# W2 and beta loaded second and multiplied first on TensorE, in a two-layer hypergraph block

## The reference

```python
def hypergraph_conv(x, adj, W, b):
    H = (adj != 0).astype(x.dtype)
    w = adj.reshape(N, -1)[:, :C]
    xw = jnp.einsum('ncd,hd->nch', x, W)
    Dn = jnp.einsum('nce,ne->nc', H, w)
    Dn = jnp.where(Dn > 0, 1.0 / Dn, 0.0)
    Be = H.sum(axis=1)
    Be = jnp.where(Be > 0, 1.0 / Be, 0.0)
    m = Be[:, :, None] * jnp.einsum('nce,nch->neh', H, xw)
    out = Dn[:, :, None] * jnp.einsum('nce,neh->nch', H, m)
    return out + b

h = jnp.maximum(_layernorm(x, axis=-1), 0.0)
a = jax.nn.relu(hypergraph_conv(h, adj, W1, b1))
a = layer_norm(a, gamma, beta)
x = x + (hypergraph_conv(a, adj, W2, b2) + h)
```

## Time and profile before

| | us |
|---|---|
| median of 3 runs (639.63 to 640.46) | 640.25 |
| the profiled execution | 639.93 |
| its span | 638.1 |
| TensorE (PE) busy | 619.6 |
| VectorE (DVE) busy | 475.1 |
| ScalarE (ACT) busy | 290.3 |
| GpSimd (POOL) busy | 110.9 |

### The profile page before, as it was taken

One profiled execution on the slowest core, in us unless ns is written; L12 is line 12 of the kernel. 1 busy time (PEld: TensorE's weight loads), 2 busy tenths in 40 slices (PEclk: granted clock), 3 DMA queues, 4 the chain that ended last, 5 costly groups with the idle time before them and its releaser, 6 DMA issues.

```text
span 638.1 us, 11993 instructions
## 1 busy us (share of the span) xinstructions
PE 619.6 (97%) x4808; PEld 467.1 (73%) x4808; DVE 475.1 (74%) x1148; ACT 290.3 (45%) x540; POOL 110.9 (17%) x132
## 2 busy tenths in 40 slices
PE   2999799999999999999999999999999999999998
PEld 1756658688586885778766886768858688586887
DVE  6899878976689765995779948798478876388632
ACT  4464935373435635364353632646335373125620
POOL 0114019422210304004040040401212012000000
PEclk9999999999999999999999999999999999999999
DMA  8995680169810696108951099213990159000701
GB/s 336 257 349 106 124 339 2 33 126 187 348 34 2 151 222 288 34 1 201 250 211 34 22 225 299 116 34 82 203 357 21 34 115 207 10 1 2 196 3 67
DMA packets 146215, 89.78 MB, mean 141 GB/s; under 512 B 134896, under 2 KB 135536, under 8 KB 141168
## 3 DMA queue, kind: packets, MB, share of 16 engines
q1 hardware_dynamic: 146160, 89.02, 51.6%
HBM read 47.06 MB, written 8.39 MB: 87 GB/s over the span
## 4 chain that ended last, share of the span: by engine, by line
PE 92%; DVE 4%; ACT 2%; DMA 1%; issue 0%
PE acc L582 18%; PE acc L599 18%; PE acc L522 15%; PE acc L563 12%; PE acc L543 11%; PE acc L502 7%; PE acc L504 7%; PE acc L484 2%; PE acc L443 1%; PE acc L445 1%; DVE z L937 1%; DMA z<-z_split_ring 1%; ACT z_split_ring L671 1%; ACT z L672 1%; DMA x_in<-x 1%; DVE incidence L873 1%
## 5 line engine op out<-in xcount | busy, mean ns | idle before, releaser
L582 PE MATMUL acc<-xw_split,incidence 128*128 128x256 f16 x1024 | 113.2, 273 | 0.0
L599 PE MATMUL acc<-edge_means,incidence_t 128*128 128x256 f16 x1024 | 113.1, 273 | 0.0
L582 PEld LDWEIGHTS acc<-xw_split,incidence 128*128 128x128 bf16 x1024 | 100.1, 98 | 13.2 <-DVE xw_split L973 0.2
L599 PEld LDWEIGHTS acc<-edge_means,incidence_t 128*128 128x128 bf16 x1024 | 100.2, 98 | 13.1
L629 ACT ACTIVATE edge_means<-acc,edge_inverse 128x256 f16<-128x256 f32 x128 | 55.2, 472 | 116.1 <-PE acc L582 68.4
L502 PE MATMUL acc<-h_split,incidence 128*128 128x257 f16 x448 | 98.6, 273 | 0.0
L504 PE MATMUL acc<-h_split,incidence 128*128 128x256 f16 x448 | 98.6, 273 | 0.0
L522 PE MATMUL acc<-incidence_t,edge_means 128*128 128x512 bf16 x448 | 97.8, 379 | 0.0
L563 PE MATMUL acc<-w_split,z 128*128 128x256 f16 x768 | 85.5, 273 | 3.5 <-DMA z<-z_split_ring 3.5
L563 PEld LDWEIGHTS acc<-w_split,z 128*128 128x128 f16 x768 | 74.9, 98 | 13.1 <-DVE edge_means L1024 2.7
L543 PE MATMUL acc<-w_split,pt_split 128*128 128x512 f16 x384 | 84.2, 379 | 0.0
(11 more groups left out here) (104 smaller groups left out, 639.4 us busy)
## 6 DMA issues: line engine op xcount, KB each, us to landing
adj_in<-adj SPq DMA_DIRECT2D x32, 1024.0 KB, 10.2
out<-residual SPq DMA_DIRECT2D x32, 256.0 KB, 2.6
x_in<-x SPq DMA_DIRECT2D x7, 1024.0 KB, 5.5
edge_weights<-adj SPq DMA_DIRECT2D x7, 512.0 KB, 3.7
x_in<-x SPq DMA_DIRECT2D x2, 512.0 KB, 4.6
z<-w1t SPq DMA_DIRECT2D x1, 512.0 KB, 12.5
xw_split<-w2t SPq DMA_DIRECT2D x1, 512.0 KB, 13.2
incidence_t<-incidence SPq DMA_TRANSPOSE x32, 4.8
```

Source lines behind the costliest of these rows:

```text
L582: last = nc.tensor.matmul(acc[:, 0:DOUT], inc[:, b.slot, ct, P * et:P * (et + 1)], xw[:, ct, part, :], start=(ct == 0 and part == HI), sto ...
L599: last = nc.tensor.matmul(acc[:, 0:DOUT], inc_t[:, b.slot, ct, et, :], edge[:, et, part, :], start=(et == 0 and part == HI), stop=(et == T ...
```

## The change

W2 and beta are issued second and third on SP, ahead of the second half of x. beta has its own semaphore, so GpSimd need not wait for gamma. `bias_times_w2` is the first work on TensorE, cut into two halves of 128 columns that go into banks 6 and 7 at columns 264 to 391, beside the sums of the first stage A (columns 0 to 256). The degrees go to bank 5. On VectorE, the inverse root of the lower half of x comes directly after its variance, two of the upper half's four `bn_stats` go behind the first `h0_lo`, the upper variance goes behind the second `h0_lo`, and `split_weights` goes behind the first `factor`.

```diff
--- before.py
+++ after.py
@@ -91,7 +91,8 @@
     Z_BEHIND = 2
     ZRING = 6
     RING = 8
-    BIAS_BANK, DEGREE_BANK = 7, 6
+    BIAS_BANK, DEGREE_BANK = 6, 5
+    BIAS_AT = LO_AT
     WPARTS = 3
     CT_FIRST = 6
     PER_BATCH = 5 * T + 4
@@ -183,6 +184,8 @@
         def u_group(b, g):
             return res[:, b.slot, GT * g:GT * (g + 1), :] if b.offset < 2 else u[:, g % 2, :, :]
 
+        bias_sums = acc_ring[:, BIAS_BANK:BIAS_BANK + 2, BIAS_AT:BIAS_AT + P]
+
         def counts(b, half):
             at = place("A", b, T // 2 * half)
             return acc_ring[:, at:at + T // 2, ONE]
@@ -193,6 +196,7 @@
         adj_loaded = [sem(f"adj_loaded{q}") for q in range(QUARTERS)]
         x_first = sem("x_first")
         weights_loaded = sem("weights_loaded")
+        beta_loaded = sem("beta_loaded")
         w1_loaded = sem("w1_loaded")
         rows_loaded = sem("rows_loaded")
         stored = [sem(f"stored{q}") for q in range(QUARTERS)]
@@ -341,14 +345,14 @@
             b0, nxt = Batch(0, 0), Batch(0, 1)
             x_rows = rows(x, b0)
             sp.dma_start(x_in[:, 0:T // 2, :], x_rows[:, 0:T // 2, :]).then_inc(x_first, 16)
+            sp.dma_start(w2f, w2t.rearrange("(t p) o -> p t o", p=P)).then_inc(w2_loaded, 16)
+            sp.dma_start(gb[:, 1, :], beta).then_inc(beta_loaded, 16)
             sp.dma_start(x_in[:, T // 2:T, :], x_rows[:, T // 2:T, :]).then_inc(x_loaded, 16)
             for q in range(QUARTERS):
                 load_adj(b0, q)
-            sp.dma_start(gb[:, 1, :], beta).then_inc(weights_loaded, 16)
             sp.dma_start(gb[:, 0, :], gamma).then_inc(weights_loaded, 16)
             sp.dma_start(w_col[:, 0, :], first_weights).then_inc(col_loaded, 16)
             sp.dma_start(w1f, w1t.rearrange("(t p) h -> p t h", p=P)).then_inc(w1_loaded, 16)
-            sp.dma_start(w2f, w2t.rearrange("(t p) o -> p t o", p=P)).then_inc(w2_loaded, 16)
             sp.dma_start(b2_row[:, :], b2.to_broadcast([P, DOUT])).then_inc(b2_loaded, 16)
             for q in range(2):
                 sp.wait_ge(inc_ready, QT * (q + 1))
@@ -398,7 +402,7 @@
                     nc.gpsimd.tensor_tensor(res[:, b.slot, t, :], x_in[:, t, :], b2_row[:, :],
                                             ALU.add).then_inc(res_ready, 1)
 
-            pool.wait_ge(weights_loaded, 32)
+            pool.wait_ge(beta_loaded, 16)
             for ht in range(HT_):
                 last = nc.gpsimd.tensor_copy(beta_cols[:, ht, :], gb[:, 1, ht:ht + 1].to_broadcast([P, P]))
             last.then_inc(beta_ready, 1)
@@ -448,11 +452,13 @@
                         last.then_inc(a_done, 1)
 
             def bias_times_w2():
+
                 pe.wait_ge(beta_ready, 1)
                 pe.wait_ge(w2_loaded, 16)
-                for ht in range(HT_):
-                    last = nc.tensor.matmul(acc_ring[:, BIAS_BANK, 0:DOUT], beta_cols[:, ht, :], w2f[:, ht, :],
-                                            start=(ht == 0), stop=(ht == HT_ - 1))
+                for half in range(2):
+                    for ht in range(HT_):
+                        last = nc.tensor.matmul(bias_sums[:, half, :], beta_cols[:, ht, :],
+                                                w2f[:, ht, P * half:P * (half + 1)], start=(ht == 0), stop=(ht == HT_ - 1))
                 last.then_inc(bias_done, 1)
 
             def first_degrees():
@@ -468,8 +474,6 @@
             def first_stage_b():
                 b = Batch(0, 0)
                 for half in range(2):
-                    if half == 1:
-                        bias_times_w2()
                     for q in (2 * half, 2 * half + 1):
                         pe.wait_ge(inc_t_ready[q], 16)
                     if half == 1:
@@ -530,10 +534,10 @@
                 for t in range(T):
 
                     pe.wait_ge(pt_ready, b.count(4, 2 * (t // 4 + 1)))
+                    if isinstance(b.loop, int) and b.offset == 0 and place("C", b, t) == BIAS_BANK:
+                        pe.wait_ge(bias_read, 1)
                     if isinstance(b.loop, int) and b.offset == 0 and place("C", b, t) == DEGREE_BANK:
                         pe.wait_ge(deg_read, 1)
-                    if isinstance(b.loop, int) and b.offset == 0 and place("C", b, t) == BIAS_BANK:
-                        pe.wait_ge(bias_read, 1)
                     if not (isinstance(b.loop, int) and b.offset == 0):
                         pe.wait_ge(t2_ready, b.next(-1).count(T, t + 1))
                     acc = bank("C", b, t)
@@ -602,6 +606,7 @@
                     last.then_inc(f_done, 1)
 
 
+            bias_times_w2()
             first_stage_a()
             first_stage_b()
             stage_c(Batch(0, 0))
@@ -755,7 +760,7 @@
             for g in range(GROUPS // 2, GROUPS):
                 relu_tiles(b0, g)
                 h0_hi_part(b0, g)
-            act.wait_ge(weights_loaded, 32)
+            act.wait_ge(weights_loaded, 16)
             act.wait_ge(w2_loaded, 16)
             for ht in range(HT_):
                 last = copy(gf[:, ht, :], w2f[:, ht, :], scale=gb[:, 0, ht:ht + 1])
@@ -1070,15 +1075,16 @@
             for t in range(T // 2):
                 V.bn_stats(stat[:, t, :], x_in[:, t, :]).then_inc(x_stat, 1)
             variance(x_ln, x_stat, x_half, b0, X_STEPS, DIN, lower)
+            inverse_root(x_ln, x_half, b0, X_STEPS, 1.0, lower)
             dve.wait_ge(x_loaded, 16)
-            for t in range(T // 2, T):
+            for t in range(T // 2, T // 2 + 2):
                 V.bn_stats(stat[:, t, :], x_in[:, t, :]).then_inc(x_stat, 1)
-                if t == T // 2 + 1:
-                    inverse_root(x_ln, x_half, b0, X_STEPS, 1.0, lower)
             incidence(b0, 0)
             h0_lo(b0, 0)
+            for t in range(T // 2 + 2, T):
+                V.bn_stats(stat[:, t, :], x_in[:, t, :]).then_inc(x_stat, 1)
+            h0_lo(b0, 1)
             variance(x_ln, x_stat, x_step, b0, X_STEPS, DIN, upper)
-            h0_lo(b0, 1)
             inverse_root(x_ln, x_step, b0, X_STEPS, 1.0, upper)
             incidence(b0, 1)
             h0_lo(b0, 2)
@@ -1088,7 +1094,6 @@
             for g in range(GROUPS):
                 ts = slice(GT * g, GT * (g + 1))
                 V.tensor_tensor(res[:, 0, ts, :], x_in[:, ts, :], res[:, 0, ts, :], ALU.add).then_inc(x_added, GT)
-            split_weights()
             dve.wait_ge(w1_loaded, 16)
             largest(0, w1f)
             dve.wait_ge(gamma_w2, 1)
@@ -1098,13 +1103,14 @@
                 for et in range(T // 2 * half, T // 2 * (half + 1)):
                     t1_lo_part(b0, et)
             factor(0, w1_scale, 1.0 / (H0_SCALE * PT_SCALE * W_SCALE))
+            split_weights()
             x_stats(nxt)
             inverse_root(x_ln, x_step, nxt, X_STEPS, 1.0)
             b_lo(b0, 0)
             b_lo(b0, 1)
             dve.wait_ge(bias_done, 1)
-            largest(2, acc_ring[:, BIAS_BANK:BIAS_BANK + 1, 0:DOUT]).then_inc(bias_step, 1)
-            V.tensor_copy(bw_row[:, :], acc_ring[:, BIAS_BANK, 0:DOUT]).then_inc(bias_read, 1)
+            largest(2, bias_sums).then_inc(bias_step, 1)
+            V.tensor_copy(bw_row[:, :].rearrange("p (a o) -> p a o", o=P), bias_sums).then_inc(bias_read, 1)
             dve.wait_ge(bias_step, 1)
             V.scalar_tensor_tensor(out=wall[:, 1:2], in0=wm[:, 2:3], scalar=BIAS_ROOM, in1=wall[:, 1:2],
                                    op0=ALU.mult, op1=ALU.max).then_inc(bias_step, 1)
```

## The result

The changed kernel takes 643.18 us (median of 21 runs, 641.32 to 645.78) and the kernel before 640.06 on the same chip (21 runs). The ratio is 1.0043 with a 95% interval of 1.0033 to 1.0053, so the change costs 3.1 us. The forecast of 640.6 with a range up to 641.8 was too low. The profiled execution of the changed kernel took 644.00 us with a span of 642.2, against 639.93 and 638.1 before.

What follows compares the result with a forecast made beforehand. Time was taken as first stage D's start plus a constant, set by VectorE's list from 45.2 us on. -0.06 (earlier start) + 0.89 (`split_weights`) - 0.14 (waiting filled) = +0.69 on 639.93 gave 640.6, range 639.0 to 641.8.

Steps and rivals of the forecast that it cites:

- What bounds the kernel: First stage D waits for transposes of z; its start plus a constant gives the time; VectorE's list sets the chain from 45.2.
- The loads: At the opening, W2 and beta ahead of `adj` cost 1.4 us: first quarter lands at 10.34 instead of 8.94.
- VectorE: Up to the edge counts: ready at 26.31, 0.06 earlier than 26.37; then `split_weights` adds 0.89, less 0.14 of waiting.
- TensorE: the step that failed: Opening: product from 9.24 to 12.55, clock up at 14.1, first stage A's release at 25.67, 0.7 sooner.
- a sign of being wrong: At the edge counts: a release by TensorE after 26.5 would show the prediction wrong.
- rival 3: First stage A: clock rises only 4.9 us after A's start, or half-width matmuls take twice as long; +1.70, 641.6; chance 0.20.
- The halves of the product: Bias product at the start, cut in halves: 3.3 us if time follows columns (taken), 6.6 if each instruction takes as before.
- The pause ahead of D: TensorE's wait ahead of the first stage D grows from 1.3 to about 4.4 us.
- rival 4: First stage D: the longer pause lets the clock fall; 640.9, or 641.4 if it stays low longer; chance 0.08.
- the gain that was to be harmless: TensorE's 1.73 us saved in stage B, ending only as a longer wait ahead of stage D.

Runs made afterwards that it cites:

- e4: Changed kernel with SP's old order of loads and the product back in stage B; VectorE's order and banks stay changed: 643.05 us, ratio 1.0044 to the kernel before.
- e1: Changed kernel with the product of beta and W2 put back between the halves of the first stage B, early loads kept: 643.55 us, ratio 1.0051.
- e6: Changed kernel with five more float32 matmuls behind the product, to close the pause ahead of stage A: 642.38 us, ratio 1.0029.
- e7: Changed kernel with the product back in stage B and 35 16-bit matmuls on ones in its old place: 640.72 us, ratio 1.0009.
- f2: Changed kernel with 40 short 16-bit matmuls added at TensorE's start, lengthening its list: 640.80 us, ratio 1.0017.
- v2: Kernel before with two GpSimd steps exchanged and 58 16-bit matmuls on ones ahead of stage A: 636.29 us, ratio 0.9935.
- after_again: Changed kernel run once more, unchanged, for a second profile: 643.42 us, one run.
- e2: Changed kernel with `split_weights` put back ahead of the two maxima: 642.53 us, ratio 1.0031.
- v1: Kernel before with two GpSimd steps exchanged (low part of W2 ahead of batch 1's residual sums): 637.29 us, ratio 0.9942.

## Why the prediction was wrong, step by step

- **What bounds the kernel.** Right up to stage D: a shift of the hand-over reaches D's start unchanged (1.52 at the hand-over, 1.52 at 72.86 against 71.34). Wrong in "the time of the whole run is the start of that stage D plus a constant". D's own length varies with the clock and with the place of a q8 packet, and the rest varies by the wait in the last D (0 to 1.77). The 5.31 that a transpose took the earlier trace rows was read as its own time; without a packet beside it, one took 3.6 to 3.7.
- **The loads.** Mis-sized: `adj` at 11.03 in place of 10.34, so A's first matmul at 13.07, where the forecast had 12.55. The DMA moved 229, 300 and 330 GB/s in the windows from 3 to 6 us, not 426. Beta came at 7.09 in place of 6.65, but GpSimd's copies took 1.00 in place of 2.59, so the product began at 8.14 in place of 9.24.
- **VectorE.** Right: it was ready for the counts at 27.21 - 0.51 = 26.70, against 26.31, and the 0.4 is what is left of `adj` coming 0.69 late. `split_weights` takes 0.90 for 0.89, and from the counts to the hand-over it is 20.17, 0.68 more than before (forecast 0.75).
- **TensorE: the step that failed.** "If the clock rises 4.9 us after 9.24, at 14.1 ... the release that VectorE waited for at 26.37 comes at 25.67." The rise came at 16.5, 3.4 after A's first matmul, and the release at 27.2, 1.5 after the forecast and past the 26.5 that the prediction had named as a sign of being wrong. The forecast let the product raise the clock for A, and A follow it without a pause. The product came 1.1 us early and A 0.5 late, with a pause of 1.15 between them. The forecast had A begin 0.95 late and win back 1.65; in the runs the early loads cost 1.60 at the counts (e4 to e1), and the product won back only 0.15 to 0.62 of it (e1 to the two profiles of the changed kernel). Why the clock did not rise ahead of A stays open: with the pause closed by more work (e6), with 16-bit work and the pause (e7), and once with the product and the pause (f2), it did. The result is the place and nearly the size of rival 3 (release 27.3, hand-over +1.70, measured +1.52), but its mechanism only in part: A's delay of 1.5 comes from the late `adj`, not from the product, and the rise came sooner after A's start than the 4.9 of rival 3. The halves of the product took 3.78, the nearer of the two bounds.
- **The pause ahead of D.** Forecast 4.4, measured 3.74. That it lets the clock fall was rival 4, with a chance of 0.08 and a price of 0.3 to 0.8; it fell in both profiles, and 19 of 21 executions have a mean clock of 0.997 or less, against 10 of the 32 of the kernel before that ran beside e1 to e4. So the chance was far too small. The price was nearer: 1.67 in the first profile, where the fall came late in D, but only 0.1 to 0.2 in the second and in e6, where it came in the pause and D's own waits took up the rest, as rival 4 had reckoned.
- **The rivals as a set.** They were priced as if one excluded the others. Rivals 3 and 4 both came, and the second followed from the same cause as the gain that was to be harmless: TensorE's 1.7 us saved in stage B lengthen the pause. In the two profiles, the lateness leaves 1.2 to 2.1 at D's end, the clock adds 0.2 to 1.7, and the remaining 1.15 to 1.33 is the packet, which nothing in the forecast foresaw. The forecast of 640.6 had 0.69 of lateness alone.

How the three parts mix over all executions isn't settled: the mean clock of an execution tells that the clock fell, not where, and the last wait is seen in profiles only. What the runs do show is that lateness and packet alone are enough for a loss of about 3 (two executions of the changed kernel and eight of e1 at a mean clock of 1.0).

## What to carry to other kernels

Work taken off an engine that waits later doesn't vanish: it lengthens that wait, and on TensorE a longer wait can cost the clock in the work behind it (here 0.1 to 1.7 us, as far as the work behind had no waits of its own to take it up). Throwaway matmuls (35 in e7, 58 in v2) brought the first stage to the full clock in both profiles; the early product did so in one of six, and its early load cost 1.6. When a change alters the length of an instruction list, look at the profile for new waits far behind the change before explaining them by it.

## What the runs showed of the hardware beyond that

- TensorE's clock fell inside pauses of 3.73 and 3.75 (after_again, e6), in the first profile of the change only after one of 3.74 and a second of 2.08, and in e1 after 1.96, 0.69 and 2.24; it stayed through 3.77 in f2 and 2.85 in e2. The length of one pause alone did not decide. The rise came 4.9 us after A's first matmul in the kernel before, 4.2 in its second profile and 4.0 in v1. The Trainium skill, page "TensorE: Matmul & The Clock Gate", section "Part 1: The HAM clock gate", says that the point of the change varies from run to run of one kernel; the rows agree.
- GpSimd's four copies of beta took 1.00 beside VectorE's small steps (0.16 to 0.22 each, at 7.18 to 8.13 in the changed kernel), and 2.59 beside `incidence` and `h0_lo`. In v1 a sum of four numbers took 0.16 where it took 2.16 beside GpSimd's subtraction. The Trainium skill, page "SBUF — State Buffer", section "Who interferes with whom", has VectorE with two inputs in SBUF and GpSimd reading SBUF get in each other's way; the sum agrees, and for the copies no run parts `h0_lo` (two inputs) from the rest.
